# An attention kernel on one core: the out-projection's first group opens the pass, and the last values product follows the first step's scores

## The chip, the core and the metric

The kernel runs on one NeuronCore of a Trainium2 chip. The metric is the device time of one execution in microseconds (us). The core has five engines with a program each: TensorE (PE; the loading of its weights is shown as PEld), VectorE (DVE), ScalarE (ACT), GpSimd (POOL) and SyncE (SP), which here issues every DMA. They run side by side and wait for each other by semaphores only.

## The reference, cut to what matters

```python
x = inputs["x"]                                # (8, 768, 32, 32): 8 images, 768 channels, N = 1024 pixels
xn = group_norm(x, G=32)
q, k, v = (einsum('oc,bchw->bohw', W, xn).reshape(8, 12, 64, 1024) for W in (Wq, Wk, Wv))
scores = einsum('bhdn,bhdm->bhnm', q, k) / 8   # 12 heads of 64 channels
out = einsum('bhnm,bhdm->bhdn', softmax(scores), v).reshape(8, 768, 32, 32)
return x + einsum('oc,bchw->bohw', Wp, out)
```

All in float32. The kernel makes up for the fast float32r format by splitting q, k, the attention's output and Wp into a high and a low part and adding three products.

## The kernel before, in words

**Two phases.** The first normalizes x and projects q, k and v to DRAM (to about 1226 us of the profiled run). The second, `attend_phase`, is the attention with the out-projection woven in. The change touches the second alone.

**Passes and steps.** The second phase handles two heads at a time, a pair; there are 48 pairs and so 48 passes, numbered p. A pass has 8 steps t of 128 keys each. PE does for each step of pair p, in an order that is written out by hand in `pair` (all loops are unrolled):

- *scores by key* (`scores_by_key`, L837): two halves h of 512 queries. A half is eight matmuls: three split products for each of the two heads, and last (c == 3) a product of ones with `top`, which adds the negative row maxima to the scores. The banks are 0 and 1 for h = 0, 2 and 7 for h = 1.
- *values* (`values`, L850): four float32 matmuls that add this step's exponentials times v into banks 5 and 6 (`heads`). In a pass they come one step late: step t issues `values(p, m, u, t - 1)`, and the values product of step 7 is issued in the next pass.
- *units* (`maxima`, `scores_by_query`, L822): two matmuls for pair p + 1, whose scores are computed once by query to get the maxima. There are 16 units in a pass, and `UNITS_BY_STEP` says how many stand at the front of a step, behind, late and at its end. Bank pair 3 and 4 is their only one, so a unit waits until DVE has reduced the one before (L985).
- *groups* (`output`, L860): from p = 8 (`LAG`) on, a pass also computes two blocks of the out-projection of an earlier image, 18 matmuls each into bank 7 (`small`), at step 0 and step 4 (`OUT_AT`). DVE adds x to it (`add_x`, L1024) and SP stores it.

**The other engines.** ACT turns the scores into `p_all` by four exponentials a step (`exponent`, L949; 0.52 us from one to the next, by four in 2.07 us), and once a pair copies `heads` to `o` (`take_heads`, L956). `p_all` holds three steps. POOL sums `p_all` over the steps (L797), divides `o` (L780) and makes its low part (L785). DVE reduces the units, and at the end of a pass joins and turns the maxima of pair p + 1 (L83, L87, L89).

**SP's queue.** In each pass SP issues, in this order: q and k of pair p + 2 (L71, L72), stores and loads of y (L697, L701), v (L672), the two parts of a finished head (L712, L714), in every third pass six loads of the out-projection's operand `a` (L706, 512 KB each), then the reciprocals of the sums to DRAM (L682), a wait for their landing, their broadcast back (L685), and last the turned maxima of pair p + 1 into `top` (L77, two DMAs, semaphore `top_in`).

**The seam.** Below, the seam of pass p is the stretch of PE between the values product of step 6 of pair p - 1 and that of step 0 of pair p. It contains the last values product of pair p - 1, group 0, three units of pair p + 1, and the scores of steps 0 and 1 of pair p. 40 passes (p = 8 to 47) have such a seam with a group in it.

Of the kernel before, what the change touches and what calls it, by code (L numbers as in the profile page):

```python
# [536 lines left out]
def attend_phase(nc, S, shared, x, q_dram, k_dram, v_dram, o_dram, recip_dram, out, psum):  # L537
    B, C, N, KT, DH, MT = S.B, S.C, S.N, S.KT, S.DH, S.MT
# [6 lines left out]
    LAG = KT + SHIFT  # L545
    SCALE = float(DH) ** -0.5
    OUT_AT = (0, MT // 2)
    UNITS_BY_STEP = ((1, 1, 1, 0),) + ((0, 0, 1, 1),) * (MT - 2) + ((0, 0, 1, 0),)
    UNITS = 2 * MT
    FINISH_AT, DIVIDE_AT, HIGH_AT, LOW_AT = 5, 1, 2, 3  # L550
    ADDS = 2 * (MT - 1)
# [8 lines left out]
    with ExitStack() as ctx:  # L560
# [7 lines left out]
        qk_in, top_in, rows_ready, max_done = shared.qk_in, shared.top_in, shared.rows_ready, shared.max_done  # L568
# [27 lines left out]
        exp_done = sem("exp_done")  # L596
# [38 lines left out]
        def at_least(p, n):  # L635

            return not known(p) or p >= n

        def before(p, n):

            return not known(p) or p < n
# [6 lines left out]

            return (p + 1, m + 1, u)

        def units(t):

            done = sum(map(sum, UNITS_BY_STEP[:t]))
            ends = [done + sum(UNITS_BY_STEP[t][:n]) for n in range(5)]
            return [range(a, z) for a, z in zip(ends, ends[1:])]

        TAIL = 2 * (NP - LAG)
# [152 lines left out]
        def _(pe):  # L810
# [13 lines left out]

            def scores_by_key(p, m, t, h):
                e = m % SLOTS
                if t == 0 and h == 0:
                    pe.wait_ge(top_in, 32 * (p + 1))
                wait(pe, exp_done, (p * MT + t) * 4 + 2 * h - 2)
                if h == 1 and t in (OUT_AT[0], OUT_AT[1] + 1) and at_least(p, LAG):  # L830
                    pe.wait_ge(y_done, (p - LAG) * 2 + (1 if t == OUT_AT[0] else 2))
                cols, keys = slice(h * BANK, (h + 1) * BANK), slice(t * P, (t + 1) * P)
                for c in range(4):
                    for i, part in enumerate(half_of):
                        left, right = ((k[e][part, 0, keys], q[e][part, 0, cols]), (k[e][part, 0, keys], q[e][part, 1, cols]),
                                       (k[e][part, 1, keys], q[e][part, 0, cols]), (ones_r[part, :], top[e][part, cols]))[c]
                        mm = pe.matmul(psum[:, SCORE_BANKS[2 * h + i], :], left, right, start=(c == 0), stop=(c == 3))  # L837
                        if c == 3:
                            mm.then_inc(s_ready, 1)
# [26 lines left out]
            def pair(p, m, u):  # L866
                first, last = known(p) and p == 0, known(p) and p == NP - 1

                def maxima(which):
                    for unit in which if not last else ():  # L870
                        scores_by_query(*after(p, m, u), unit)

                def group(s):
                    n = 2 * (m - LAG) + s
                    if s == 1:
                        pe.wait_ge(exp_done, (p * MT + OUT_AT[1] + 1) * 4)
                    wait(pe, y_done, (p - LAG) * 2 + s)
                    output(small, n % KT, PRODUCTS, (2 * (p - LAG) + s) // KT + 1 if u is None else u * (2 * BODY // KT) + (n // KT + 1))

                for t in range(MT):  # L880
                    front, behind, late, end = units(t)
                    maxima(front)
                    if t == 0:
                        if not first:
                            values(p - 1, m - 1, None, MT - 1)
                        if at_least(p, LAG):
                            group(0)
                    maxima(behind)
                    scores_by_key(p, m, t, 0)
                    scores_by_key(p, m, t, 1)  # L890
                    maxima(late)
                    if t > 0:
                        values(p, m, u, t - 1)
                    if t == OUT_AT[1] and at_least(p, LAG):
                        group(1)
                    maxima(end)
# [41 lines left out]
        @block.scalar  # L938
        def _(act):
            def exponent(p, m, t, h):  # L940
                n = p * MT + t
                for i in range(2):
                    if h == 0:
                        back = t - EXPS
                        if i == 0:
                            wait(act, pv_done, n - EXPS + 1)
                        wait(act, added, p * ADDS + (2 * max(back, 1) if back >= 0 else 2 * back + 2) - 1 + i)
                    act.wait_ge(s_ready, n * 4 + 2 * h + i + 1)
                    act.activation(p_all[:, i, (m * MT + t) % EXPS, h * BANK:(h + 1) * BANK], psum[:, SCORE_BANKS[2 * h + i], :], ACT.Exp,  # L949
                                   scale=SCALE).then_inc(exp_done, 1)  # L950

            def take_heads(p, m):

                act.wait_ge(pv_done, (p + 1) * MT)
                wait(act, o_lo_done, p - 1)
                act.copy(o[:, m % 2, :], heads.rearrange("p a n -> p (a n)")).then_inc(un_done, 1)  # L956

            def high_out(p, m, hi=o_hi[:]):
                act.wait_ge(o_done, p + 1)
                wait(act, o_out, 32 * min(p, NP - 2) if known(p) else 32 * p)  # L960
                act.copy(hi, o[:, m % 2, :]).then_inc(o_hi_done, 1)

            def pair(p, m, u):
                first = known(p) and p == 0
                for t in range(MT):
                    if t == 0 and not first:
                        take_heads(p - 1, m - 1)
                    exponent(p, m, t, 0)
                    exponent(p, m, t, 1)
                    if t == HIGH_AT and at_least(p, 2):  # L970
                        high_out(p - 2, m - 2)

            all_pairs(act, pair)
            take_heads(NP - 1, NP - 1)
            for kt in range(KT - 2, KT):
                high_out(NP - KT + kt, NP - KT + kt, a_last[kt][:, 0, :])

        @block.vector
        def _(dve):
# [40 lines left out]
            def add_x(n, s, count, bank=small):  # L1020

                dve.wait_ge(kt_done, (n + 1) * KT)
                dve.wait_ge(x_in[s], 16 * count)
                dve.tensor_tensor(y[:, s, :], bank, y[:, s, :], ALU.add).then_inc(y_done, 1)  # L1024
# [5 lines left out]
            def pair(p, m, u):  # L1030
                first, last = known(p) and p == 0, known(p) and p == NP - 1
                for t in range(MT):
                    front, behind, late, end = units(t) if not last else [()] * 4
                    for unit in front:
                        unit_max(p + 1, m + 1, unit)
                    if t == OUT_AT[0] and at_least(p, LAG):
                        add_x((p - LAG) * 2, 0, p - LAG + 1)
                    for unit in (*behind, *late):
                        unit_max(p + 1, m + 1, unit)
                    if t == MT - 1 and not last:  # L1040
# [72 lines left out]
```

## Time and profile before

| | |
|---|---|
| time, median of 3 runs (lowest, highest) | 3361.74 us (3361.03, 3362.54) |
| time of the profiled execution | 3362.28 us |
| its span | 3360.5 us |
| busy share: PE, PEld, DVE, ACT, POOL | 99%, 67%, 53%, 32%, 55% |
| granted TensorE clock over the span | 0.999 |
| DMA, mean busy share of the 16 engines by queue 1 | 39.2% |

A row of the timeline is a run of equal instructions on one engine: its start and length in us, the engine, line, operation and operands, how many, and in brackets how long the engine was idle before it and what ended that. PE's matmul rows have modelled ends, so lengths of work on PE are taken below from the starts of the PEld rows, one of which stands before every matmul. A PEld row regularly starts some tenths of a us before its matmul, and a short idle time on PEld is no loss as long as PE streams.

### The profile page before, as it was taken

To read this page: it belongs to the slowest core of one execution; us is meant where nothing else is said; L and a number is where in the kernel's file an instruction comes from. 1 tells how busy PE (TensorE), PEld (TensorE's weight loads), DVE (VectorE), ACT (ScalarE), POOL (GpSimd) and SP (SyncE) were. 2 spreads that over 40 slices of the span, in tenths; PEclk is the share of its full clock that TensorE was granted. 3 is DMA by queue.
4 is the path that set the end of the run, shared out by engine and by line. 5 is a ranking of instruction groups with operands and counts; after the bars stand their busy time and mean duration, and the time that the engine had idled before them with its cause. 6 is when DMAs were issued, how large, how long until landed. Compare 5 with 4: busy or idle time off the path is not lost.

```text
span 3360.5 us, 47732 instructions
## 1 busy us (share of the span) xinstructions
PE 3312.3 (99%) x18272; PEld 2248.3 (67%) x18272; DVE 1781.8 (53%) x2417; ACT 1089.0 (32%) x1945; POOL 1837.6 (55%) x793
## 2 busy tenths in 40 slices
PE   7999999999999999999999999999999999999999
PEld 6888888888888864445555555555555555555557
DVE  4333323233233247776666666666666666666652
ACT  3111111111111124554444444444444444444441
POOL 2000000000000039999888888888888888888883
PEclk9999999999999999999999999999999999999999
DMA  6333333423242432333434434444344343343434
GB/s 232 110 139 107 144 124 132 148 103 138 102 146 107 159 113 99 123 142 129 164 120 151 145 118 153 141 148 157 126 164 154 121 156 134 121 164 129 155 107 169
DMA packets 221602, 461.57 MB, mean 137 GB/s; under 512 B 22896, under 2 KB 72944, under 8 KB 220144
## 3 DMA queue, kind: packets, MB, share of 16 engines
q1 hardware_dynamic: 221424, 459.16, 39.2%
q8 instruction: 116, 1.90, 0.2%
q14 instruction: 62, 0.51, 0.0%
HBM read 259.06 MB, written 199.62 MB: 136 GB/s over the span
## 4 chain that ended last, share of the span: by engine, by line
PE 56%; issue 3%; DMA 1%; ACT 1%; POOL 1%; DVE 1%; SPq 0%; ACTq 0%; POOLq 0%
PE psum L850 19%; PE psum L837 19%; PE psum L860 10%; PE psum L822 6%; PE psum L915 1%; ACT p_all L949 1%; POOL sums L797 1%; DMA recip_rows<-compact 1%; DMA w_second<-turned 1%; DVE half_max L985 0%; SPq L685 0%; SPq L77 0%; DVE flip L997 0%; POOL o L780 0%; DVE flipped L87 0%
## 5 line engine op out<-in xcount | busy, mean ns | idle before, releaser
L797 POOL TENSOR_TENSOR sums<-sums,p_all 128x1024 f32<-128x1024 f32 x576 | 1353.1, 2389 | 0.0
L985 DVE TENSOR_REDUCE half_max<-psum 128x2 f32<-128x1024 f32 x752 | 921.2, 1225 | 492.3 <-PE psum L822 486.7
L949 ACT ACTIVATE p_all<-psum 128x512 f32<-128x512 f32 x1536 | 792.8, 602 | 948.6 <-PE psum L837 946.7
L850 PE MATMUL psum<-p_all,v 128*64 128x512 f32 x3072 | 743.4, 605 | 0.0
L416 POOL MEMSET x_first<- 128x1024 f32 x1 | 1.0, 956 | 1067.6 <-PE psum L340 1067.6
L837 PE MATMUL psum<-w_second 64*128 64x512 f32 x3072 | 446.1, 395 | 12.6 <-DMA w_second<-turned 5.9
L850 PEld LDWEIGHTS psum<-p_all,v 128*64 128x64 f32 x3072 | 186.3, 136 | 351.7 <-issue 249.5
L392 ACT CAST stage<-psum 128x512 fp32r<-128x512 f32 x192 | 112.7, 588 | 952.8 <-PE psum L340 943.1
L505 DVE TENSOR_TENSOR stage<-psum,stage 128x512 fp32r<-128x512 f32 x192 | 132.6, 692 | 530.0 <-ACT stage L392 529.8
L797 POOL TENSOR_TENSOR sums<-p_all 128x1024 f32<-128x1024 f32 x96 | 226.9, 2386 | 309.5 <-ACT p_all L949 309.5
L860 PE MATMUL psum<-a,w_first 128*128 128x512 f32 x1512 | 367.5, 397 | 0.0
L860 PEld LDWEIGHTS psum<-a,w_first 128*128 128x128 f32 x1512 | 277.5, 188 | 121.5 <-issue 33.3
L837 PEld LDWEIGHTS psum<-w_second 64*128 64x128 f32 x3072 | 282.7, 184 | 92.2 <-ACT p_all L949 28.5
L822 PE MATMUL psum<-w_second 64*128 64x512 f32 x1024 | 230.0, 444 | 6.3 <-DVE neg_max L1027 4.0
L822 PEld LDWEIGHTS psum<-w_second 64*128 64x128 f32 x1024 | 96.0, 184 | 202.3 <-DVE half_max L985 142.7
L837 PE MATMUL psum<-x_first 64*128 64x512 f32 x1536 | 224.1, 397 | 3.6 <-DMA x_first<-turned 2.1
L510 DVE COPY stage<-psum 128x384 f32<-128x384 f32 x128 | 71.3, 557 | 250.3 <-PE psum L340 250.3
L340 PE MATMUL psum<-w_third,x_second 128*128 128x384 f32 x1152 | 203.2, 335 | 0.0
L340 PE MATMUL psum<-w_third,x_first 128*128 128x384 f32 x1152 | 202.8, 335 | 0.0
L837 PE MATMUL psum<-x_first,ones_r 64*128 64x512 f32 x1024 | 201.8, 389 | 0.0
L340 PEld LDWEIGHTS psum<-w_third,x_second 128*128 128x128 f32 x1152 | 199.7, 188 | 2.5 <-issue 2.0
L340 PEld LDWEIGHTS psum<-w_third,x_first 128*128 128x128 f32 x1152 | 199.8, 188 | 0.6
(88 smaller groups left out, 3263.5 us busy)
## 6 DMA issues: line engine op xcount, KB each, us to landing
q_parts<-stage SPq DMA_DIRECT2D x192, 256.0 KB, 2.2
k_parts<-stage SPq DMA_DIRECT2D x192, 256.0 KB, 2.3
a<-o_parts SPq DMA_DIRECT2D x84, 512.0 KB, 7.8
w_second<-q_parts SPq DMA_DIRECT2D x32, 1024.0 KB, 5.2
w_second<-k_parts SPq DMA_DIRECT2D x32, 1024.0 KB, 7.6
v_rows<-stage SPq DMA_DIRECT2D x128, 192.0 KB, 2.1
v<-v_rows SPq DMA_DIRECT2D x48, 512.0 KB, 4.5
recip_all<-recip_rows SPq DMA_DIRECT2D x96, 256.0 KB, 3.8
```

What stands on the lines that cost most here:

```text
L340: mm = pe.matmul(out, lhs, rhs, start=(kt == 0 and n == 0), stop=(kt == KT - 1 and n == 2))
L392: act.copy(stage[:, r, 0:BANK], psum[:, r, :]).then_inc(hi_done, 1)
L505: dve.tensor_tensor(stage[:, r, BANK:2 * BANK], psum[:, r, :], f32(stage[:, r, 0:BANK]), ALU.subtract).then_inc(lo_done, 1)
L510: dve.tensor_copy(f32(stage[:, r, 0:VC]), psum[:, r, 0:VC]).then_inc(lo_done, 1)
L797: pool.tensor_tensor(sums[:, m % 2, i, :], first, p_all[:, i, n, :], ALU.add).then_inc(added, 1)
L822: mm = pe.matmul(rows[:, i, :], queries, k[e][part, 0, h * BANK:(h + 1) * BANK], start=True, stop=True)
L837: mm = pe.matmul(psum[:, SCORE_BANKS[2 * h + i], :], left, right, start=(c == 0), stop=(c == 3))
L850: mm = pe.matmul(heads[part, h, :], v[:, e, t, part], p_all[:, i, (m * MT + t) % EXPS, cols], start=(t == 0), stop=(t == MT - 1))
L860: mm = pe.matmul(bank, wp[:, wpart, kt, ot * P:(ot + 1) * P], a_of[kt][:, apart, :], start=first, stop=final)
L915: mm = pe.matmul(psum[:, LAST_BANKS[n], :], wp[:, wpart, kt, ot * P:(ot + 1) * P], a_last[kt][:, apart, half * BANK:(half + 1) * BANK], st ...
L949: act.activation(p_all[:, i, (m * MT + t) % EXPS, h * BANK:(h + 1) * BANK], psum[:, SCORE_BANKS[2 * h + i], :], ACT.Exp, scale=SCALE).then ...
L985: dve.tensor_reduce(half_max[:, :, t, h], rows, AX.X, ALU.max, negate=True).then_inc(max_done, 1)
```

## The change

In passes with an out-projection (p >= 8) group 0 is issued first, ahead of the first unit. The last values product of pair p - 1 is issued behind the scores of step 0 and the unit that now follows them; one more unit stands behind it. ACT's copy of `heads` moves behind the four exponentials of step 0, and DVE's `add_x` ahead of the first unit's reduction. The wait for the maxima (`top_in`) moves, in all passes, from the first matmul of step 0's scores to the first that reads `top` (c == 3). Group 0 now waits itself for all exponentials of the pass before, since it overwrites bank 7.

```diff
--- before.py
+++ after.py
@@ -546,6 +546,7 @@
     SCALE = float(DH) ** -0.5
     OUT_AT = (0, MT // 2)
     UNITS_BY_STEP = ((1, 1, 1, 0),) + ((0, 0, 1, 1),) * (MT - 2) + ((0, 0, 1, 0),)
+    UNITS_WITH_OUT = ((1, 0, 1, 1),) + UNITS_BY_STEP[1:]
     UNITS = 2 * MT
     FINISH_AT, DIVIDE_AT, HIGH_AT, LOW_AT = 5, 1, 2, 3
     ADDS = 2 * (MT - 1)
@@ -648,10 +649,11 @@
 
             return (p + 1, m + 1, u)
 
-        def units(t):
-
-            done = sum(map(sum, UNITS_BY_STEP[:t]))
-            ends = [done + sum(UNITS_BY_STEP[t][:n]) for n in range(5)]
+        def units(p, t):
+
+            steps = UNITS_WITH_OUT if at_least(p, LAG) else UNITS_BY_STEP
+            done = sum(map(sum, steps[:t]))
+            ends = [done + sum(steps[t][:n]) for n in range(5)]
             return [range(a, z) for a, z in zip(ends, ends[1:])]
 
         TAIL = 2 * (NP - LAG)
@@ -824,13 +826,13 @@
 
             def scores_by_key(p, m, t, h):
                 e = m % SLOTS
-                if t == 0 and h == 0:
-                    pe.wait_ge(top_in, 32 * (p + 1))
                 wait(pe, exp_done, (p * MT + t) * 4 + 2 * h - 2)
                 if h == 1 and t in (OUT_AT[0], OUT_AT[1] + 1) and at_least(p, LAG):
                     pe.wait_ge(y_done, (p - LAG) * 2 + (1 if t == OUT_AT[0] else 2))
                 cols, keys = slice(h * BANK, (h + 1) * BANK), slice(t * P, (t + 1) * P)
                 for c in range(4):
+                    if t == 0 and h == 0 and c == 3:
+                        pe.wait_ge(top_in, 32 * (p + 1))
                     for i, part in enumerate(half_of):
                         left, right = ((k[e][part, 0, keys], q[e][part, 0, cols]), (k[e][part, 0, keys], q[e][part, 1, cols]),
                                        (k[e][part, 1, keys], q[e][part, 0, cols]), (ones_r[part, :], top[e][part, cols]))[c]
@@ -872,25 +874,25 @@
 
                 def group(s):
                     n = 2 * (m - LAG) + s
-                    if s == 1:
-                        pe.wait_ge(exp_done, (p * MT + OUT_AT[1] + 1) * 4)
+                    pe.wait_ge(exp_done, (p * MT + (OUT_AT[1] + 1 if s == 1 else 0)) * 4)
                     wait(pe, y_done, (p - LAG) * 2 + s)
                     output(small, n % KT, PRODUCTS, (2 * (p - LAG) + s) // KT + 1 if u is None else u * (2 * BODY // KT) + (n // KT + 1))
 
                 for t in range(MT):
-                    front, behind, late, end = units(t)
+                    front, behind, late, end = units(p, t)
+                    if t == 0 and at_least(p, LAG):
+                        group(0)
                     maxima(front)
-                    if t == 0:
-                        if not first:
-                            values(p - 1, m - 1, None, MT - 1)
-                        if at_least(p, LAG):
-                            group(0)
+                    if t == 0 and not first and before(p, LAG):
+                        values(p - 1, m - 1, None, MT - 1)
                     maxima(behind)
                     scores_by_key(p, m, t, 0)
                     scores_by_key(p, m, t, 1)
                     maxima(late)
                     if t > 0:
                         values(p, m, u, t - 1)
+                    elif at_least(p, LAG):
+                        values(p - 1, m - 1, None, MT - 1)
                     if t == OUT_AT[1] and at_least(p, LAG):
                         group(1)
                     maxima(end)
@@ -963,10 +965,12 @@
             def pair(p, m, u):
                 first = known(p) and p == 0
                 for t in range(MT):
-                    if t == 0 and not first:
+                    if t == 0 and not first and before(p, LAG):
                         take_heads(p - 1, m - 1)
                     exponent(p, m, t, 0)
                     exponent(p, m, t, 1)
+                    if t == 0 and at_least(p, LAG):
+                        take_heads(p - 1, m - 1)
                     if t == HIGH_AT and at_least(p, 2):
                         high_out(p - 2, m - 2)
 
@@ -1030,11 +1034,11 @@
             def pair(p, m, u):
                 first, last = known(p) and p == 0, known(p) and p == NP - 1
                 for t in range(MT):
-                    front, behind, late, end = units(t) if not last else [()] * 4
+                    front, behind, late, end = units(p, t) if not last else [()] * 4
+                    if t == OUT_AT[0] and at_least(p, LAG):
+                        add_x((p - LAG) * 2, 0, p - LAG + 1)
                     for unit in front:
                         unit_max(p + 1, m + 1, unit)
-                    if t == OUT_AT[0] and at_least(p, LAG):
-                        add_x((p - LAG) * 2, 0, p - LAG + 1)
                     for unit in (*behind, *late):
                         unit_max(p + 1, m + 1, unit)
                     if t == MT - 1 and not last:
```

What stands in a row on PE at the seam of p = 9, before (L822 is a unit, L837 scores, L850 a values product, L860 a group):

```order
L850 MATMUL psum<-p_all,v 64x512 x4
L822 MATMUL psum<-w_second 128x512 x2
L850 MATMUL psum<-p_all,v 64x512 x4
L860 MATMUL psum<-a,w_first 128x512 x18
L822 MATMUL psum<-w_second 128x512 x2
L837 MATMUL psum<-x_first 128x512 x6
L837 MATMUL psum<-x_first,ones_r 128x512 x2
L837 MATMUL psum<-x_first 128x512 x6
L837 MATMUL psum<-x_first,ones_r 128x512 x2
L822 MATMUL psum<-w_second 128x512 x2
```

And in the changed kernel, where the lines have moved by two (L824, L839, L852, L862):

```order
L852 MATMUL psum<-p_all,v 64x512 x4
L862 MATMUL psum<-a,w_first 128x512 x18
L824 MATMUL psum<-w_second 128x512 x2
L839 MATMUL psum<-x_first 128x512 x6
L839 MATMUL psum<-x_first,ones_r 128x512 x2
L839 MATMUL psum<-x_first 128x512 x6
L839 MATMUL psum<-x_first,ones_r 128x512 x2
L824 MATMUL psum<-w_second 128x512 x2
L852 MATMUL psum<-p_all,v 64x512 x4
L824 MATMUL psum<-w_second 128x512 x2
```

The values product between unit and group has gone to a place between the second and the third unit; group and first unit have changed places. The number and kind of instructions is the same.

Where PE waits for the maxima at the same seam, before, from the unit behind the group:

```order
L822 MATMUL psum<-w_second 128x512 [waits max_done]
L822 MATMUL psum<-w_second 128x512
L837 MATMUL psum<-x_first 128x512 [waits exp_done,top_in]
L837 MATMUL psum<-x_first 128x512 x5
L837 MATMUL psum<-x_first,ones_r 128x512 x2
L837 MATMUL psum<-x_first 128x512 [waits y_done,exp_done]
```

And in the changed kernel:

```order
L824 MATMUL psum<-w_second 128x512 [waits max_done,qk_in1]
L824 MATMUL psum<-w_second 128x512
L839 MATMUL psum<-x_first 128x512 [waits exp_done]
L839 MATMUL psum<-x_first 128x512 x5
L839 MATMUL psum<-x_first,ones_r 128x512 [waits top_in]
L839 MATMUL psum<-x_first,ones_r 128x512
L839 MATMUL psum<-x_first 128x512 [waits y_done,exp_done]
```

Six of the eight matmuls of the first half no longer wait for `top_in`. Of the seam's work, the values product is no longer ahead of this wait.

ACT at the same seam, before (L956 is the copy of `heads`) and in the changed kernel (L951 and L958):

```order
L949 ACTIVATE p_all<-psum 128x512 [waits s_ready,added]
L949 ACTIVATE p_all<-psum 128x512 [waits s_ready] x2
L956 COPY o<-psum 128x1024 [waits o_lo_done,pv_done]
L949 ACTIVATE p_all<-psum 128x512 [waits s_ready,added,pv_done]
L949 ACTIVATE p_all<-psum 128x512 [waits s_ready,added]
```

```order
L951 ACTIVATE p_all<-psum 128x512 [waits s_ready] x2
L951 ACTIVATE p_all<-psum 128x512 [waits s_ready,added,pv_done]
L951 ACTIVATE p_all<-psum 128x512 [waits s_ready,added]
L951 ACTIVATE p_all<-psum 128x512 [waits s_ready] x2
L958 COPY o<-psum 128x1024 [waits o_lo_done,pv_done]
L951 ACTIVATE p_all<-psum 128x512 [waits s_ready,added,pv_done]
```

The copy waits for the last values product and has moved from before the exponentials of step 0 to before those of step 1.

## Rows read from the trace of the kernel before

**Rows 1.** The chain of waits from 1600 to 3300 us, by line.

```profile
by line: PE psum L850 32.4%; PE psum L837 31.5%; PE psum L860 18.5%; PE psum L822 10.8%; issue 1.6%; ACT p_all L949 1.6%; DMA recip_rows<-compact 1.5%; DMA w_second<-turned 0.8%; DVE half_max L985 0.4%; SPq L685 0.3%; SPq L77 0.2%; POOL o L
```

**Rows 2.** The view of waits, same stretch: who waited for what, us in total, times, longest.

```profile
PEld psum L837 <- DMA w_second<-turned: 6.2, 7, 1.7
```

**Rows 3.** The timeline, the seam of p = 24.

```profile
2232.66 0.19 PEld L822 LDWEIGHTS psum<-w_second 64*128 64x128 f32 x2 [0.81 <-issue]
...
2233.62 1.39 SPq L77 DMA_DIRECT2D x_first<-turned  x2
...
2234.96 3.95 PEld L860 LDWEIGHTS psum<-a,w_first 128*128 128x128 f32 x18 [0.81 <-issue]
...
2235.07 1.02 ACT L956 COPY o<-psum 128x1024 f32<-128x1024 f32 x1 [3.19 <-PE psum L850]
...
2239.26 0.18 PEld L822 LDWEIGHTS psum<-w_second 64*128 64x128 f32 x2 [0.35 <-issue]
...
2239.37 0.65 PEld L837 LDWEIGHTS psum<-x_first 64*128 64x128 f32 x6
...
2240.07 0.19 PEld L837 LDWEIGHTS psum<-x_first,ones_r 64*128 64x128 f32 x2
...
2240.80 2.07 ACT L949 ACTIVATE p_all<-psum 128x512 f32<-128x512 f32 x4 [4.71 <-PE psum L837]
...
2241.94 0.53 PEld L837 LDWEIGHTS psum<-x_first 64*128 64x128 f32 x6 [0.51 <-ACT p_all L949]
...
2244.27 0.20 PEld L850 LDWEIGHTS psum<-p_all,v 128*64 128x64 f32 x4 [0.35 <-ACT p_all L949]
```

**Rows 4.** The timeline, an ordinary step behind it.

```profile
2246.24 0.66 PEld L837 LDWEIGHTS psum<-x_first 64*128 64x128 f32 x6
...
2247.70 2.07 ACT L949 ACTIVATE p_all<-psum 128x512 f32<-128x512 f32 x4 [2.37 <-PE psum L837]
...
2248.67 0.20 PEld L850 LDWEIGHTS psum<-p_all,v 128*64 128x64 f32 x4 [0.36 <-ACT p_all L949]
...
2250.53 0.19 PEld L822 LDWEIGHTS psum<-w_second 64*128 64x128 f32 x2 [0.81 <-DVE half_max L985]
```

**Rows 5.** The timeline, step 4 of the same pass.

```profile
2257.41 0.20 PEld L850 LDWEIGHTS psum<-p_all,v 128*64 128x64 f32 x4 [0.35 <-ACT p_all L949]
...
2259.28 3.99 PEld L860 LDWEIGHTS psum<-a,w_first 128*128 128x128 f32 x18 [0.81 <-ACT p_all L949]
```

**Rows 6.** The timeline, the seam of p = 14.

```profile
1786.73 0.32 SPq L682 DMA_DIRECT2D recip_rows<-compact  x1
...
1788.82 0.19 PEld L822 LDWEIGHTS psum<-x_first 64*128 64x128 f32 x2 [0.81 <-issue]
...
1793.45 1.39 SPq L77 DMA_DIRECT2D w_second<-turned  x2
...
1797.35 0.53 PEld L837 LDWEIGHTS psum<-w_second 64*128 64x128 f32 x6 [1.74 <-DMA w_second<-turned]
...
1802.13 0.20 PEld L850 LDWEIGHTS psum<-p_all,v 128*64 128x64 f32 x4 [0.37 <-ACT p_all L949]
```

**Rows 7.** The timeline, seams of p = 11, 20 and 44.

```profile
1656.62 0.19 PEld L822 LDWEIGHTS psum<-x_first 64*128 64x128 f32 x2 [0.81 <-issue]
...
1659.50 1.39 SPq L77 DMA_DIRECT2D w_second<-turned  x2
...
2059.85 1.39 SPq L77 DMA_DIRECT2D w_second<-turned  x2
...
2063.12 0.53 PEld L837 LDWEIGHTS psum<-w_second 64*128 64x128 f32 x6 [0.94 <-DMA w_second<-turned]
...
3116.37 0.19 PEld L822 LDWEIGHTS psum<-x_first 64*128 64x128 f32 x2 [0.81 <-issue]
...
3119.30 1.39 SPq L77 DMA_DIRECT2D w_second<-turned  x2
```

**Rows 8.** Stretches: us, busy and count by engine, granted clock, DMA share, GB/s.

```profile
1226.00:1236.00 10.00, 7.06 (x34) 5.33 (x36) 3.88 (x5) 2.43 (x5) 0.00 (x0) 0.66 0.78 300
```

## The prediction

> **What bounds the kernel now.** I read the table first: PE is busy for 99% of the span at a granted clock of 0.999, and no other engine is above 55%. Then the chain of waits over the passes with an out-projection: it runs almost wholly through PE's lines, and what else it names is small: the exponentials 1.6%, the landing of the reciprocals 1.5%, the landing of the turned maxima 0.8% [rows 1]. So only what PE streams and what makes it stand still counts. The change leaves the instructions of PE as they are. It can gain or lose in the 40 seams alone, through waits, and the reader is to look there with the timeline. Call S the moment at which PE has done the values product of step 6 and goes on, before with the first unit.
>
> **An undisturbed seam before.** In the seam of p = 24, S is 2232.66, and the values product of step 0 starts at 2244.27, 11.61 us later [rows 3]. Within it the second half of the work is not tight: behind the scores of step 0 stands one unit only, and the scores of step 1 need the exponentials of step 0, which ACT begins at 2240.80; the weight load at 2241.94 has been held for 0.51 us by them [rows 3]. An ordinary step has no such hold, since a values product stands between: there 2.43 us go from the start of the scores to the values product (2246.24 to 2248.67), 1.86 for the product (to 2250.53), and 0.11 for a unit ahead of the scores, as at 2239.26 to 2239.37 [rows 3, 4].
>
> **The same seam after.** Group 0 starts at S. A group takes 4.30 us (2234.96 to 2239.26) [rows 3]; the unit adds 0.11; scores of step 0 and a unit 2.43; the values product 1.86; a unit 0.11; scores of step 1 and a unit 2.43. The sum is 11.24 instead of 11.61: 0.37 us gained, because the values product now covers the exponentials of step 0. In 40 seams that is 14.8 us. Bounds: the whole hold of 0.51 from above; from below half of it, 0.25, since a weight load runs ahead of its matmul and part of a hold passes unfelt. I take 0.37, the difference of the two sums.
>
> What could take this back is covered. Group 0's new wait for the exponentials of step 7: group 1 has stood in exactly this place, behind a values product and with that wait, and starts 1.87 us behind the product's start (2257.41 to 2259.28), like the unit in an ordinary step (1.86) [rows 4, 5]. So it costs nothing. ACT's copy takes 1.02 us and starts 0.11 behind the end of the product [rows 3]; after, the product ends at S + 8.70, the copy runs from 8.8 to 9.8, and the exponentials of step 1 cannot start before 1.46 us behind their scores' start (2246.24 to 2247.70) [rows 4], that is at S + 8.81 + 1.46 = 10.3. Slack 0.4 us. The values product of step 0, which waits for the copy, stands at S + 11.2: slack 1.4. DVE's add and first reduction keep their order against PE's first two units, only both swapped, at no cost. SP's load of v for the next pair waits for the last values product, but in SP's queue it stands behind a store of y and the wait for that store's landing anyway. POOL's sums begin with the exponentials of step 1, and from step 1 on every engine keeps its distance to PE: nothing changes towards the next seam.
>
> **The wait that comes forward.** The maxima must be in `top`. Before, all of the first half's scores waited for them: needed at 2239.37, S + 6.71 [rows 3]. After, only the ones product waits, 0.70 behind the start of the scores (2239.37 to 2240.07), but the values product has gone from ahead of it: needed at S + 4.30 + 0.11 + 0.70 = 5.11. The deadline is 1.6 us earlier. In most seams that is harmless: SP starts L77 at 2233.62, S + 0.96 [rows 3], and with 3.3 to 3.9 us from there until PE is let go (below) the maxima are there at S + 4.3 to 4.9.
>
> Every third seam (p = 11, 14 to 47, thirteen of them) is different. In the pass ahead SP has issued six loads of `a`; the reciprocals, issued at 1786.73, land so late that L77 starts at 1793.45, when S was 1788.82: S + 4.63 [rows 6]. In the twelve such seams up to p = 44 the start of L77 lies 2.9 to 4.6 us behind S, 3.6 on average (first 1656.62 and 1659.50, last 3116.37 and 3119.30, both 2.9) [rows 6, 7]. Where PE visibly waited, it went on 3.90 us (1793.45 to 1797.35) or 3.27 us (2059.85 to 2063.12) behind the start of L77 [rows 6, 7]; the other waits lie between, and I take 3.5. So in these seams the maxima are there at S + 7.1 on average. Before, that cost little: the waits of PEld for them sum to 6.2 us in 7 seams [rows 2], of which a little is not felt: at p = 14 PE went on at S + 8.53 instead of 6.71, 1.82 later, and the seam is 13.31 long (1788.82 to 1802.13), 1.70 over 11.61, so 0.12 passes under the load's lead [rows 3, 6]. I take 5.5. After, each of the 13 waits 7.1 - 5.11 = 2.0, less that 0.12: 1.87, together 24.3 us. The change does not shift L77 against S.
>
> **The sum.** -14.8 + 24.3 - 5.5 = +4.0 us. Against the profiled execution (3362.28 us, span 3360.5) that is 3366.3; the median of the runs is 0.5 below that execution, so 3365.7, a little slower. Bounds: with 3.27 for the landing and 0.51 for the gain, -20.4 + 21.3 - 5.5 = -4.6; with 3.90 and 0.25, -10.0 + 29.5 - 5.5 = +14.0.
>
> **The rivals.**
>
> *Faster: the late seams do not get dearer.* If the maxima come correspondingly earlier in the changed kernel, the 14.8 us stay. The mechanism would be SP's chain: POOL's low part of the head is what starts the loads of `a`, and if POOL gets ahead of PE by 1 us or more, the reciprocals find the queues free. Against it: POOL starts each pass from PE's own scores of step 1, and both ends of that distance move together. In full, 3361.7 - 14.8 = 3347; half of it, 3355.
>
> *No change because the landing is shorter.* What PE's waits show are the late cases alone; if the other six land in under 3.27 us behind L77, by about 0.3, 2 us go, and with a gain of 0.42 a seam another 2: 3361.7. This joins the forecast's lower side.
>
> *Slower: the clock.* The stall at p = 14 becomes 8.53 - 5.11 = 3.4 us of idle PE. At the start of the second phase PE is busy for 7.06 of the 10 us from 1226 to 1236, and the granted clock there is 0.66 [rows 8]: the lower level, 1.2 GHz, for 6.8 of them, which costs 3.4 us. The long waits of before (1.74 at p = 14) left it at 2.4 GHz (0.999 over the span). If two to four stalls bring the clock down, 7 to 14 us more come on top: 3373 to 3380. It decides from a stall between 1.7 and some 3 us; only seams nearly as late as that of p = 14 come near.
> The Trainium skill (TensorE: Matmul & The Clock Gate, "HAM oscillation — how this bites in real kernels") warns of just this, a DMA wait between stretches of matmuls that lets the clock fall and makes the next stretch start cold; by that rule the longest stalls are the places to look at. This trace agrees as far as it goes, with one fall, at the pause between the phases, and none at 1.74 us.
>
> *Slower: ACT's copy is late.* If the last values product's end reaches ACT 0.4 us later than I work out, the exponentials of step 1 slip and with them the scores of step 2; 0.4 us in 40 seams take the gain away: 3365.7 + 15 = 3381. Against it is the slack of 0.4 us from rows of the same instructions.
>
> **How the numbers follow.** The forecast 0.68 (its own range 3359 to 3373), the late seams staying cheap 0.13, the clock 0.12, ACT's copy or another new hold 0.07. What a measurement can tell from no change is 0.2%, 6.7 us: faster is under 3355.0, slower over 3368.5. Of the forecast's 0.68 about 0.50 lie within, 0.16 above, 0.02 below; of the cheap late seams 0.09 are faster and 0.04 the same; clock and copy count as slower, but for 0.04. So faster 0.11, same 0.58, slower 0.31. The range runs from 3356 to 3374; the cases outside it hold about 0.2.
>
> **What would show it.** In the changed profile: in undisturbed seams 11.2 us from the group's first weight load to the values product of step 0, no hold by exponentials on the scores of step 1, and pass after pass 43.7 us instead of 44.1. In every third seam the ones product (L839) waits for the turned maxima for 1.2 to 3.4 us, and the waits of PEld for them sum to 24 to 26 us instead of 6.2. ACT's copy lies between the exponentials of steps 0 and 1 with idle time behind it. The granted clock stays at 1.00 behind the longest stall. I am wrong if the waits for the maxima sum to under 15 us, if other seams have them too, or if the ordinary step, 4.4 us, has changed its length.

## The result, and the profile after

The changed kernel takes 3370.64 us (median of 10 runs, 3368.4 to 3374.48), the kernel before 3361.61 us (10 runs, 3358.7 to 3363.86): a ratio of 1.0028, 95% interval 1.0020 to 1.0036. It is 9.0 us slower where 4 were forecast; the time lies in the range. The profiled execution took 3373.42 us, 2.8 over the median, with a span of 3371.6 and a granted clock of 0.997 where there was 0.999 before.

The chain of waits over the same stretch as before [rows 1]; each name with its share:

```profile
by line: PE psum L852 31.8%; PE psum L839 31.1%; PE psum L862 15.2%; PE psum L824 11.1%; DMA recip_rows<-compact 3.9%; DMA w_second<-turned 2.2%; DVE half_max L989 1.2%; SPq L687 1.0%; SPq L77 0.7%; issue 0.6%; DMA x_first<-turned 0.5%; DVE
```

The landings of the reciprocals and of the maxima have grown from 1.5% and 0.8% to 3.9% and 2.2% (with 0.5% more for the maxima that go into `x_first`), and the exponentials, 1.6% before, are under 0.5% and no longer in the list. The view of waits, to be read against the 6.2 us in 7 waits of before [rows 2]:

```profile
PEld psum L839 <- DMA w_second<-turned: 27.5, 13, 3.2
PEld psum L839 <- DMA x_first<-turned: 2.5, 4, 0.8
```

The first row is the 13 seams of every third pass: 27.5 us. The second is four more waits, at p = 12, 13, 30 and 31, in seams that had none before. The seam of p = 24, to be read against [rows 3]:

```profile
2236.17 3.96 PEld L862 LDWEIGHTS psum<-a,w_first 128*128 128x128 f32 x18 [0.81 <-ACT p_all L951]
...
2237.14 1.39 SPq L77 DMA_DIRECT2D x_first<-turned  x2
...
2240.48 0.19 PEld L824 LDWEIGHTS psum<-w_second 64*128 64x128 f32 x2 [0.35 <-issue]
...
2240.59 0.65 PEld L839 LDWEIGHTS psum<-x_first 64*128 64x128 f32 x6
...
2241.29 0.19 PEld L839 LDWEIGHTS psum<-x_first,ones_r 64*128 64x128 f32 x2
...
2242.99 0.20 PEld L852 LDWEIGHTS psum<-p_all,v 128*64 128x64 f32 x4 [0.33 <-ACT p_all L951]
...
2244.98 1.01 ACT L958 COPY o<-psum 128x1024 f32<-128x1024 f32 x1 [0.89 <-PE psum L852]
...
2246.42 2.07 ACT L951 ACTIVATE p_all<-psum 128x512 f32<-128x512 f32 x4 [0.43 <-PE psum L839]
...
2247.39 0.20 PEld L852 LDWEIGHTS psum<-p_all,v 128*64 128x64 f32 x4 [0.36 <-ACT p_all L951]
```

From the group at 2236.17 to the values product of step 0 at 2247.39 are 11.22 us; 11.61 were before and 11.24 forecast. The ones product stands at 2241.29, S + 5.12. ACT's copy ends at 2245.99, 0.43 before the exponentials of step 1. Every term of the undisturbed seam is as worked out. The seam of p = 14, against [rows 6]:

```profile
1785.25 0.32 SPq L684 DMA_DIRECT2D recip_rows<-compact  x1
...
1787.33 3.99 PEld L862 LDWEIGHTS psum<-a,w_first 128*128 128x128 f32 x18 [0.81 <-ACT p_all L951]
...
1790.33 1.15 SPq L687 DMA_DIRECT2D recip_all<-recip_rows  x2
...
1791.53 1.39 SPq L77 DMA_DIRECT2D w_second<-turned  x2
...
1795.20 0.29 PEld L839 LDWEIGHTS psum<-w_second,ones_r 64*128 64x128 f32 x2 [2.77 <-DMA w_second<-turned]
...
1795.36 1.19 PEld L839 LDWEIGHTS psum<-w_second 64*128 64x128 f32 x6
...
1796.64 0.33 PEld L839 LDWEIGHTS psum<-w_second,ones_r 64*128 64x128 f32 x2
...
1798.05 0.29 PEld L852 LDWEIGHTS psum<-p_all,v 128*64 128x64 f32 x4 [0.65 <-issue]
```

The reciprocals' store of 1785.25 has landed by 1790.33; only then comes L77, at S + 4.20, and PEld waits 2.77 us for the maxima. The rows behind it are the new thing: those of weight loads for the ones and the values products take 0.29 to 0.33 us instead of 0.19 or 0.20, from 1795.20 to 1798.05. The stretches that show it (columns as in [rows 8]):

```profile
1787.00:1795.00 8.00, 5.87 (x28) 3.97 (x26) 2.92 (x8) 0.00 (x0) 6.14 (x3) 1.00 0.47 133
1795.00:1799.00 4.00, 3.80 (x16) 2.27 (x18) 0.83 (x1) 2.17 (x4) 0.00 (x0) 0.57 1.00 374
2064.00:2069.00 5.00, 5.00 (x22) 1.74 (x22) 1.23 (x1) 2.37 (x5) 0.00 (x0) 0.66 0.98 363
2464.00:2468.00 4.00, 4.00 (x18) 1.62 (x14) 1.23 (x1) 2.17 (x4) 0.00 (x0) 0.57 1.02 375
```

A granted clock of 0.57 over 4 us is 3.4 us at the lower level, 1.2 GHz, which costs 1.7. The trace has four such falls, behind the waits of p = 14, 20, 29 and 35 (the last three rows above are at p = 14, 20 and 29), of 2.8, 3.2, 2.2 and 3.1 us. The wait of p = 38 has none, and its weight load is back at 0.19 us at once; so the length of the wait alone does not decide:

```profile
2867.84 0.19 PEld L839 LDWEIGHTS psum<-w_second,ones_r 64*128 64x128 f32 x2 [2.31 <-DMA w_second<-turned]
```

**Where the time went.** I measured all 40 seams from the PEld rows, here from the values product of step 6 to that of step 0 (13.48 us undisturbed before, 13.10 after; the seam of p = 47 has no units and is some 1 us shorter), and set the 13 late ones apart. Everything behind the seams of passes 8 to 47 has the same length in all kernels, 1222 us within 0.4.

| profiled execution, us | 27 other seams | 13 late seams | PEld's waits for maxima | lost to the clock |
|---|---|---|---|---|
| before | 363.9 | 179.7 | 6.2 | 0 |
| changed | 355.4 | 200.8 | 30.0 | 6.8 |
| changed, L77 first | 353.7 | 169.3 | 0 | 0 |
| before, L77 first | 363.9 | 174.2 | 0 | 0 |
| changed, wait at the first product | 359.3 | 211.6 | 40.3 | 10.2 |
| before, wait at the ones product | 363.9 | 174.7 | 0.8 | 0 |
| group first only | 364.5 | 176.6 | 2.0 | 0 |
| changed, half of `a` | 354.2 | 169.4 | 1.2 | 0 |
| new order only where p % 3 is not 2 | 355.9 | 175.3 | 4.2 | 0 |
| filled, 8 matmuls | 356.1 | 198.3 | 2.8 | 0 |
| filled, 4 matmuls | 355.6 | 193.7 | 12.6 | 0 |

The last three kernels treat every pass from p = 8 on with p % 3 == 2 alike, so p = 8 too, which is not one of the 13 late seams. It stands in the first column, with 13.48, 15.34 and 14.38 us instead of the 13.1 of the changed kernel.

Between the first two rows lie +12.6 us: the order gains 10.2 + 4.9 = 15.1 (rows three and four against each other), waits go from 5.5 to 26.4 (1.7 of it outside the late seams), and the clock takes 6.8. The passes before p = 8 give 1.3 back. The spans differ by 11.1, the medians of the runs by 9.0.

### The profile page after: what moved, and what is told of

Read it like the earlier page. It is cut to its first block, busy times and chain, and to the rows that moved or that the text cites. A ratio compares the mean times of both kernels' runs of the same rounds, so it can differ in the third digit from the quotient of the medians.

```text
span 3371.6 us, 47712 instructions
## 1 busy us (share of the span) xinstructions
PE 3310.6 (98%) x18272; PEld 2252.2 (67%) x18272; DVE 1781.3 (53%) x2417; ACT 1089.2 (32%) x1945; POOL 1838.1 (55%) x793
## 4 chain that ended last, share of the span: by engine, by line
PE 54%; DMA 4%; issue 2%; DVE 1%; SPq 1%; POOL 1%; ACT 0%; ACTq 0%; POOLq 0%
PE psum L852 19%; PE psum L839 19%; PE psum L862 9%; PE psum L824 7%; DMA recip_rows<-compact 2%; PE psum L917 1%; DMA w_second<-turned 1%; DVE half_max L989 1%; POOL sums L799 1%; SPq L687 1%; SPq L77 0%; DMA x_first<-turned 0%; ACT p_all L951 0%; DVE compact L1022 0%; DVE flip L1001 0%
## 5 line engine op out<-in xcount | busy, mean ns | idle before, releaser
L951 ACT ACTIVATE p_all<-psum 128x512 f32<-128x512 f32 x1536 | 793.1, 602 | 1040.3 <-PE psum L839 894.2
L852 PE MATMUL psum<-p_all,v 128*64 128x512 f32 x3072 | 747.4, 607 | 0.0
L839 PE MATMUL psum<-w_second 64*128 64x512 f32 x3072 | 442.4, 392 | 0.9 <-ACT p_all L951 0.4
L852 PEld LDWEIGHTS psum<-p_all,v 128*64 128x64 f32 x3072 | 187.1, 136 | 358.9 <-issue 243.0
L862 PE MATMUL psum<-a,w_first 128*128 128x512 f32 x1512 | 367.8, 397 | 0.0
L862 PEld LDWEIGHTS psum<-a,w_first 128*128 128x128 f32 x1512 | 277.5, 188 | 121.9 <-ACT p_all L951 64.9
L839 PEld LDWEIGHTS psum<-w_second 64*128 64x128 f32 x3072 | 288.5, 185 | 64.1 <-ACT p_all L951 9.3
L824 PE MATMUL psum<-w_second 64*128 64x512 f32 x1024 | 230.5, 445 | 8.5 <-DVE half_max L989 4.5
L824 PEld LDWEIGHTS psum<-w_second 64*128 64x128 f32 x1024 | 96.2, 184 | 204.8 <-DVE half_max L989 166.4
L839 PE MATMUL psum<-x_first 64*128 64x512 f32 x1536 | 222.2, 394 | 0.2
L839 PE MATMUL psum<-x_first,ones_r 64*128 64x512 f32 x1024 | 202.9, 391 | 2.6 <-DMA x_first<-turned 2.6
```

Source lines behind the costliest of these rows:

```text
L824: mm = pe.matmul(rows[:, i, :], queries, k[e][part, 0, h * BANK:(h + 1) * BANK], start=True, stop=True)
L852: mm = pe.matmul(heads[part, h, :], v[:, e, t, part], p_all[:, i, (m * MT + t) % EXPS, cols], start=(t == 0), stop=(t == MT - 1))
L862: mm = pe.matmul(bank, wp[:, wpart, kt, ot * P:(ot + 1) * P], a_of[kt][:, apart, :], start=first, stop=final)
```

## The experiments

**L77 ahead of the reciprocals' wait.** SP's only edit, in the changed kernel and in the kernel before: `spread_recip` keeps the store, and its wait for the landing and the broadcast become `broadcast_recip`:

```diff
                 if at_least(p, 1):
                     spread_recip(p - 1)
                 if not (known(p) and p == NP - 1):
                     maxima(p + 1, m + 1)
+                if at_least(p, 1):
+                    broadcast_recip(p - 1)
```

> The changed kernel, but SP issues the turned maxima (L77) ahead of its wait for the reciprocals and of their broadcast. My theory: the 3.4 ms kernel lost time only because in every third seam the maxima reach `top` later than the deadline, which the change put 1.6 us earlier. Then L77 starts 0.96 us behind S in all seams, the maxima are there by S + 4 to 5, the waits for them vanish, the clock never falls, and what stays is the gain of 0.38 us in 40 seams: about 3340 us (3336 to 3345). Rival A: the loss comes from elsewhere (the group in front, the later copy of `heads`, the later load of v): then it stays near 3370. Rival B: the small transfer queues behind the loads of `a` wherever it is issued: L77 starts early but the maxima still land at S + 6 or later in every third seam, and the time falls by a few us only, to 3362 to 3368.

> The kernel before with the same move of L77 ahead of the reciprocals' broadcast. My theory: only its own 5.4 us of waits in late seams go: 3356 us (3353 to 3358), far less than the 30 us that the same move is to give the changed kernel. Rival A says no gain in either. Rival B: 3359 to 3362.

Measured: 3338.48 us (5 runs, ratio to the kernel before 0.9932, 95% interval 0.9918 to 0.9945) and 3356.41 us (11 runs, 0.9982, 0.9973 to 0.9991), both as expected. Rival A is out: without the late maxima the changed kernel is 18 us faster than the same repair of the kernel before. Rival B is out by the timeline of the repaired changed kernel at p = 14, where the reciprocals are as late as ever:

```profile
1781.50 0.32 SPq L684 DMA_DIRECT2D recip_rows<-compact  x1
...
1783.58 3.99 PEld L867 LDWEIGHTS psum<-a,w_first 128*128 128x128 f32 x18 [0.81 <-ACT p_all L956]
...
1784.54 1.40 SPq L77 DMA_DIRECT2D w_second<-turned  x2
...
1786.52 1.14 SPq L689 DMA_DIRECT2D recip_all<-recip_rows  x2
...
1788.73 0.19 PEld L844 LDWEIGHTS psum<-w_second,ones_r 64*128 64x128 f32 x2
```

The store of 1781.50 again needs 5.0 us until the broadcast at 1786.52, but L77 has started at S + 0.96, and the ones product at 1788.73 (S + 5.15) has no wait in its row. This is the fastest of all kernels here, 0.7% under the kernel before.

**The deadline moved by 0.7 us either way.**

```diff
-                if t == 0 and h == 0:
-                    pe.wait_ge(top_in, 32 * (p + 1))
...
                 for c in range(4):
+                    if t == 0 and h == 0 and c == 3:
+                        pe.wait_ge(top_in, 32 * (p + 1))
```

Undone in the changed kernel, and done alone in the kernel before:

> The changed kernel with the wait for the maxima back at the first matmul of step 0's scores, 0.70 us earlier than in the changed kernel. My theory: each of some 17 late seams waits 0.7 us more (12 us), the seven seams before the out-projection lose 0.3 us each again, and since the pauses are longer the clock falls in more of them than four, at 1.7 us each: 3384 to 3395. Rival A: the deadline is not what matters, within 3 us of 3371.

> The kernel before with only the wait for the maxima moved to the first product that reads `top`. My theory: a deadline 0.7 us later leaves about 2 of the 5.4 us of waits in late seams, and gains 0.3 us in each of the seven early seams: 3361.6 - 3.3 - 2 = 3356 (3354 to 3358). If the split wait costs something of its own (one more wait between products that accumulate in one bank), it stays at 3360 to 3362.

Measured: 3389.35 us (5 runs, 1.0086, 1.0073 to 1.0100), and 3355.62 us (11 runs, 0.9982, 0.9973 to 0.9991). The first is 19 us over the changed kernel: its waits grow to 40.3 us in 19 seams, and the clock falls six times, for 10.2 us instead of 6.8. Waits of 2.5 to 3.4 us were followed by a fall, waits of up to 2.3 were not. The second shows that the moved wait costs nothing and is worth 5.0 us in the late seams (179.7 to 174.7) by itself, where I had expected 3.3. In the early passes my 0.3 us a seam was mostly wrong: the seven seams get 4.2 us shorter, but the passes give 3.0 back. So it was luck that the sum fell into its range. In those passes DVE waits longer for POOL, 6.1 us instead of 3.0 in the kernel before, as the view of waits from 1240 to 1520 us of this kernel shows:

```profile
DVE flip L997 <- POOL sums L797: 6.1, 5, 1.5
```

POOL needs 16 operations of 2.39 us, 38 us, for a pass, and an early pass of this kernel takes 35.7 to 37.7 us: there POOL cannot keep up, and most of what PE gains at the seam it loses behind it.

**The group first, without moving the values product.**

```diff
-    UNITS_WITH_OUT = ((1, 0, 1, 1),) + UNITS_BY_STEP[1:]
+    UNITS_WITH_OUT = ((1, 1, 1, 0),) + UNITS_BY_STEP[1:]
...
                     maxima(front)
-                    if t == 0 and not first and before(p, LAG):
+                    if t == 0 and not first:
                         values(p - 1, m - 1, None, MT - 1)
```

> One half of the change: group 0 stands first in the pass, but the last values product stays ahead of step 0's scores (behind the first unit); the wait for the maxima is at the ones product. My theory: gain and loss of the change both come from where the values product stands, and the place of the group is neutral. Then the deadline is S + 7.4 as in the kernel before with the wait at the ones product (3355.6 us), the scores of step 1 are held by the exponentials again, and the time is that kernel's: 3354 to 3358. Rival: the group in front has a price or a gain of its own, then it is off by over 3 us.

Measured: 3359.24 us (11 runs, 0.9990, 0.9981 to 0.9999), 3.6 over the kernel before with the wait at the ones product, and 1.2 above the range that I expected. Its timeline at p = 24 has both of the old properties:

```profile
2229.80 3.96 PEld L862 LDWEIGHTS psum<-a,w_first 128*128 128x128 f32 x18 [0.81 <-ACT p_all L949]
...
2237.22 0.19 PEld L839 LDWEIGHTS psum<-x_first,ones_r 64*128 64x128 f32 x2
...
2239.09 0.53 PEld L839 LDWEIGHTS psum<-x_first 64*128 64x128 f32 x6 [0.53 <-ACT p_all L949]
...
2241.43 0.20 PEld L852 LDWEIGHTS psum<-p_all,v 128*64 128x64 f32 x4 [0.37 <-ACT p_all L949]
```

The ones product is at S + 7.42, the exponentials hold the scores of step 1, and the seam is 11.63 us. So the group's place gains nothing. By my own measure, over 3 us off, the rival holds: this order has a small price. Of the 3.6 us, 1.9 lie in the late seams, 0.6 in the others and 1.4 in the first phase, which the edit does not touch; so some 2.5 us belong to the order, and what causes them was not tested.

**Half the bytes of `a`.** From the third use of each part of `a` on only the high part is brought; the low part's products use old data.

```diff
+                if used > 1:
+                    sp.dma_start(f32(a_of[kt][:, 0:1, :]), o_dram[0:1, ...]...).then_inc(a_in[kt], 16)
+                    return
```

> The changed kernel, with SP's queue in its own order, but the later loads of `a` bring the high part alone: half the bytes, and the products with the low part use what an earlier load left there. My theory: it is these loads that delay the landing of the reciprocals and with it L77 in every third seam. Halved, they end before the reciprocals are issued, L77 starts at S + 1 nearly everywhere, and the waits and clock falls go: 3338.5 (the kernel with L77 ahead) + about 3 for the early seams = 3340 to 3345. Rival: the delay comes from what precedes them (the stores of the finished head), then the late seams stay and the time is 3360 or more.

Measured: 3340.63 us (5 runs, 0.9936, 0.9923 to 0.9950). SP at the seam of p = 14:

```profile
1773.89 2.69 SPq L709 DMA_DIRECT2D a<-o_parts  x6
...
1782.06 0.32 SPq L684 DMA_DIRECT2D recip_rows<-compact  x1
...
1783.57 1.15 SPq L687 DMA_DIRECT2D recip_all<-recip_rows  x2
...
1785.09 1.39 SPq L77 DMA_DIRECT2D w_second<-turned  x2
```

The broadcast follows the store by 1.51 us instead of 5, and no late seam waits any more. So the bytes of the six loads ahead of the store were the cause.

**Two checks of the sum.** L77 first with the wait back at the first product; and the kernel before with L77 first and the wait at the ones product, by the diffs above:

> The changed kernel with L77 ahead of the reciprocals' broadcast, and the wait for the maxima at the first scores matmul. The maxima land 2.51 us behind the start of L77, that is at S + 3.47, and the deadline is S + 4.4 now. My theory: no wait in nearly all of the 40 seams, only the seven early seams lose 0.4 to 0.5 us each: 3338.5 + 3.5 = 3342 (3340.5 to 3344). If the split wait was worth more than these seven, 3345 or more.

> The kernel before with both repairs: L77 ahead of the broadcast and the wait at the ones product. No seam from p = 8 on waits for maxima, so it differs from the changed kernel with L77 ahead (3338.5) by the place of the values product and the group alone. My theory: 40 seams at 0.38 us, so 3338.5 + 15.2 = 3353.7 (3352.5 to 3355). If it comes out under 3350, part of the change's gain was the maxima's and not the order's.

Measured: 3340.47 us (5 runs, 0.9935, 0.9922 to 0.9949) and 3355.49 us (11 runs, 0.9981, 0.9972 to 0.9990), the second 0.5 above its range. The first has no wait from p = 8 on and is 2.0 us slower than the same kernel with the wait at the ones product, not 3.5; in the profiles the passes before p = 8 account for 1.4 of it, since POOL holds them as in the experiment above. The second lies 17.0 over the changed kernel with L77 first, where 15.2 were expected; in the profiles the seams differ by 15.1, and the other 2 us are not explained. So the gain in the seams is the order's.

**The new order only where the maxima are early.**

```diff
+        def moved(p):
+            return at_least(p, LAG) and p % 3 != 2
```

with `moved(p)` in place of `at_least(p, LAG)` for the order at step 0 on PE, ACT and DVE, and the old order otherwise. The condition leaves out p = 8 too, so the new order stands in 26 seams and not in the 27 of my sum, a difference of 0.4 us.

> The changed kernel, but the 13 seams whose maxima are late (p % 3 == 2) keep the order of the kernel before; SP's queue is left as it was. My theory: gain and loss of the change sit in different seams. The 27 other seams gain 0.38 us each, the 13 behave as in the kernel before with the wait at the ones product (3355.6): 3355.6 - 10.3 + about 1.5 for the two or three other seams whose maxima come a little late = 3346.8 (3344.5 to 3348.5), and the clock never falls. Rival: if the order itself, alternating or not, upsets what follows, it is above 3350.

Measured: 3347.77 us (5 runs, 0.9955, 0.9942 to 0.9969), within 1 us. Gain and loss sit in different seams and add.

**Filling the pause.** Matmuls whose result is not used, before the wait for the maxima; eight, and four in a second kernel. By its condition the edit fills 14 seams: the 13 late ones, and also p = 8, which has no wait to fill:

```diff
+                    if t == 0 and h == 0 and c == 3 and p >= LAG and p % 3 == 2:
+                        for _ in range(8):
+                            pe.matmul(psum[:, SCORE_BANKS[2], :], wp[:, 0, 0, 0:P], k[e][:, 0, 0:BANK], start=True, stop=True)
```

> The changed kernel, in whose 13 late seams PE first does eight matmuls (128 x 512, into bank 2, which the next scores overwrite; their result is used nowhere) and then waits for the maxima. They take 8 x 0.23 = 1.9 us of the wait's 1.3 to 3.2 us. My theory: the same waits ended by the same landings, but the pauses of PE are short, so that the four falls of the clock (1.7 us each, 6.8 us) do not come: 3370.6 - 6.8 + about 1 where the maxima are there before the eight are through = 3365 (3363 to 3367). Rival: the lower clock has cost nothing that the waits had not cost, or comes for another reason: 3370 to 3373.

> As the kernel with eight filling matmuls in the 13 late seams, but with four. The eight removed all falls of the clock, yet held the ones product until 7.5 us behind the group's start, later than most landings, and so cost some 4 us of their own. Four end at about S + 6.5, before nearly all landings (6.7 to 8.3), and leave pauses of at most 1.8 us. My theory: the falls stay away or nearly so and the filling costs nothing: 3370.6 - 6.8 + 0.5 = 3364 (3362.5 to 3366.5). Rival: the falls were not worth 1.7 us each: 3369 to 3372.

Measured: 3372.54 us with eight (7 runs, 1.0030, 1.0019 to 1.0042), a miss by 7.5 us, and 3366.57 us with four (11 runs, 1.0012, 1.0003 to 1.0021), 0.07 above the end of my range. In both the falls are gone. The row of the eight at p = 14, between the scores and the wait:

```profile
1788.88 3.97 PEld L865 LDWEIGHTS psum<-a,w_first 128*128 128x128 f32 x18 [0.81 <-ACT p_all L954]
...
1794.33 1.68 PEld L836 LDWEIGHTS psum<-w_second,w_first 128*128 128x128 f32 x8 [0.37 <-issue]
...
1796.42 0.19 PEld L842 LDWEIGHTS psum<-w_second,ones_r 64*128 64x128 f32 x2 [0.41 <-DMA w_second<-turned]
```

They begin at S + 5.45 and hold the ones product until S + 7.5, so they cost time of their own wherever the maxima land sooner, and 2.2 us at p = 8 for nothing. So this time says little about the clock. With four, the waits for the maxima in the late seams from 1600 to 3300 us are these:

```profile
PEld psum L842 <- DMA w_second<-turned: 11.5, 12, 1.7
```

No wait of PEld is over 1.7 us, no fall occurs, and the late seams take 193.7 us instead of 200.8. So 56 matmuls more, of no use to the result, made the kernel 4.1 us faster by the medians (4.3 when each kernel is taken against the kernel before of its own runs: +4.7 instead of +9.0), although the filling at p = 8 costs 1.3. The late seams of the profiles give 7.1. With the 1.3 added back, the medians put the clock's share at 5 to 6 us; the profiled run, the second longest of its ten, has 6.8. The ten runs of the changed kernel had granted clocks from 0.998 (3368.4 us) to 0.996 (3374.48), so the number of falls probably differs from run to run; only the one profile shows it.

## Why the prediction was right in its mechanism and low in its size

- The undisturbed seam: 11.24 us forecast, 11.22 measured; in 40 seams -14.8 us forecast, -15.1 measured. Right, and with it the covers: group 0's new wait, ACT's copy with a slack of 0.4, DVE's swap.
- The earlier deadline in every third seam: the 13 late seams and their waits were named, at 24.3 us against 5.5. Measured 24.7 against 5.5 there. Right.
- "In most seams that is harmless": nearly. Four seams outside the 13 waited, for 2.5 us in PEld and 1.7 in the seams' lengths. I had looked for lateness only where it was already visible.
- "The change does not shift L77 against S": it held on the mean of the late seams (S + 3.6 both times, up to p = 44), but not at p = 12, 13 and 31, where L77 started at S + 1.8 to 2.3 instead of S + 0.96 (below). At p = 30 it already started at S + 2.3 before, which the slack hid.
- The step that failed is the clock, which got a chance of 0.12 beside the forecast's 0.68. I treated the forecast and the rival as alternatives. They are one chain: the stalls that the forecast itself worked out, up to 3.4 us, were longer than any that the trace had shown to be harmless (1.7 us), so a part of the rival's price belonged in the sum. The rival had the number of falls right (two to four; the profile has four) and the size of one twice too large (3.4 us for 1.7), since it took the fall between the phases for its measure. That its lower end, 7 us, comes close to the 6.8 of the profile is luck. With +5 to +7 the forecast would have been 3371 to 3373.
- That 3370.64 lies inside the stated range is in part luck too: the range's upper end was worked out from longer landings, not from the clock. And two of the signs that the prediction gave for being wrong came true: other seams waited too, and the granted clock did not stay at 1.00. Undisturbed passes took the 43.7 us that it gave.
- The Trainium skill (TensorE: Matmul & The Clock Gate, "HAM oscillation — how this bites in real kernels") warned of a DMA wait that makes the next stretch start at the low clock. The traces agree with that warning. The page's example has waits of some 3 to 5 us; here one of 2.2 us was already followed by a fall, while one of 2.3 was not.
- Forgotten: the wait at the ones product also shortens the seven early seams. It was worth 1.3 us in the passes before p = 8, since POOL holds them.
- Of the rivals, "the late seams do not get dearer" and "ACT's copy is late" are refuted by the seams; "shorter landing" too, with a mean wait of 2.1 us in the 13.

## What to carry to other kernels

Before a work item is moved off the front of a wait, work out the deadline of every transfer behind that wait, for the worst pass of the period and not the usual one; here 27 seams gained 0.38 us each and 13 lost 21 together. A queue that waits for one transfer's landing delays every transfer behind it: issuing the urgent one first was worth 32 us on the changed kernel and 5 to 6 on the old one, so a repair may pay mainly beside the change that needs it. And when a forecast makes PE's pauses longer than any in the trace, put the lower clock into the sum.

## What was not expected of the hardware

**Four falls of equal length.** Each lasted 3.41 us at the lower level, against 6.83 between the phases. Waits of PEld of 2.2, 2.8, 3.1 and 3.2 us came before a fall in the changed kernel; 2.3 and 2.1 did not.

**A small store beside an instruction fetch.** The reciprocals' 8 KB land in 1.4 us when nothing is ahead of them. At p = 12 in the changed kernel no load of `a` is near, and they took 3.1 us. The DMA view of that stretch, 1697 to 1700 us:

```profile
q8 instruction: 1, 0.02, 2.8%
q1 hardware_dynamic: 80, 0.01, 2.1%
recip_rows<-compact SPq DMA_DIRECT2D x1, 8.0 KB, 3.1
```

A 16 KB packet of the instruction queue falls into it, which the same store of the kernel before does not have. I counted over the traces of all thirteen kernels. Outside the 13 late seams, 33 of these stores had such a packet begin between 0.3 us before and 1.35 us behind their issue, and every one of them took 2.4 to 3.3 us; the other 396 took 2.1 at most, 1.35 in the median. Which passes are hit differs from kernel to kernel: 12, 13, 30 and 31 in the changed kernel, 12, 28, 45 and 46 with the wait at the first product. No experiment separates the packet from other causes, but if it is the cause, any edit can move waits of about 1 us from one pass to another.
